# Graph-network kernel, attention pass: the next group's query-row matmuls go ahead of the second half's strip sums on TensorE

## What is computed

```python
Q, K, V = (h @ Wq), (h @ Wk), (h @ Wv)            # 8 heads of 32
score = einsum('ehd,ehd->eh', Q[dst], K[src]) / sqrt(32)
score = score + relu(efeat @ W1 + b1) @ W2 + b2
ex    = exp(score - segment_max(score, dst)[dst])
alpha = ex / segment_sum(ex, dst)[dst]
out   = segment_sum(alpha[:, :, None] * V[src], dst)
x     = layernorm(x + out @ Wo + bo)
```

## Times and profile before

| | us |
|---|---|
| median of 3 executions | 3339.93 |
| lowest and highest of them | 3326.34, 3346.44 |
| the profiled execution, its own time | 3330.41 |
| its span, first to last instruction | 3328.6 |
| part of the span in which groups of the attention pass run | about 130 to 843.5 |

### The profile page before, as it was taken

One profiled execution on the slowest core, in us unless ns is written; L12 is line 12 of the kernel. 1 busy time (PEld: TensorE's weight loads), 2 busy tenths in 40 slices (PEclk: granted clock), 3 DMA queues, 4 the chain that ended last, 5 costly groups with the idle time before them and its releaser, 6 DMA issues.

```text
span 3328.6 us, 64436 instructions
## 1 busy us (share of the span) xinstructions
PE 2517.7 (76%) x18326; PEld 1946.3 (58%) x18430; DVE 1968.7 (59%) x6179; ACT 685.5 (21%) x1593; POOL 1739.7 (52%) x1779
## 2 busy tenths in 40 slices
PE   7688888887556555567667675777777799999997
PEld 6344444444355555555555554666566488888875
DVE  3498988888655555466666666676777511111222
ACT  3244444444100000101111111111111311111110
POOL 0476555553377777677777775777777100000000
PEclk9899999999587878778888887898888799999998
DMA  5898777774133333333333332333333123322221
GB/s 188 247 267 243 218 211 213 216 214 133 53 108 110 110 109 110 99 106 114 117 118 106 116 117 79 121 117 117 121 114 120 65 99 104 103 98 91 92 91 62
DMA packets 185642, 435.94 MB, mean 131 GB/s; under 512 B 42868, under 2 KB 89322, under 8 KB 185578
## 3 DMA queue, kind: packets, MB, share of 16 engines
q0 software_dynamic: 93184, 272.74, 28.3%
q1 hardware_dynamic: 88794, 159.17, 14.8%
q10 hardware_dynamic: 3600, 3.28, 0.3%
HBM read 390.51 MB, written 44.51 MB: 131 GB/s over the span
## 4 chain that ended last, share of the span: by engine, by line
PE 32%; POOL 25%; issue 20%; DVE 12%; DMA 6%; DVEq 1%; ACT 1%; SPq 1%; POOLq 0%; ACTq 0%
POOL gath L769 25%; PE banks L1417 17%; PE banks L1260 4%; DMA gath<-h_table,idx_slot 3%; PE banks L1307 2%; PE banks L1243 2%; DVE prod L1758 2%; PE banks L1318 1%; PE banks L1083 1%; PE banks L1195 1%; DVE rh L1762 1%; PE banks L1319 1%; DVE rh L1786 1%; PE banks L1246 1%; DMA misc<-counts 1%
## 5 line engine op out<-in xcount | busy, mean ns | idle before, releaser
L769 POOL DMA_INDIRECT gath<-h_table,idx_slot x1248 | 1285.0, 1030 | 371.2 <-issue 342.3
L1260 PE MATMUL banks<-onehot,gath 128*128 128x128 f32 x4992 | 776.2, 322 | 458.1 <-DMA gath<-h_table,idx_slot 429.9
L1260 PEld LDWEIGHTS banks<-onehot,gath 128*128 128x128 f32 x4992 | 725.7, 231 | 515.9 <-DMA gath<-h_table,idx_slot 424.4
L1417 PE MATMUL banks<-gath,misc 128*128 128x256 bf16 x1875 | 515.6, 275 | 0.0
L1417 PE MATMUL banks<-acc,misc 128*128 128x256 bf16 x2500 | 419.7, 276 | 21.3 <-DMA misc<-counts 12.0
L1318 PE MATMUL banks<-gath 128*128 128x512 bf16 x624 | 251.5, 426 | 75.0 <-DVE gath L1964 74.8
L1417 PEld LDWEIGHTS banks<-acc,misc 128*128 128x128 bf16 x2500 | 242.5, 98 | 68.5 <-issue 16.1
L767 POOL DMA_INDIRECT rh<-kv_table,idx_slot x208 | 218.5, 1050 | 121.9 <-PE banks L1234 66.5
L767 POOL DMA_INDIRECT gath<-kv_table,idx_slot x208 | 211.0, 1014 | 124.0 <-PE banks L1234 68.5
L1964 DVE TENSOR_SCALAR gath<-w_qkv 128x800 bf16<-128x800 f16 x728 | 257.3, 422 | 0.0
L1844 DVE TENSOR_TENSOR acc<-acc,banks 128x256 f32 x156 | 65.0, 417 | 324.3 <-PE banks L1260 323.9
(11 more groups left out here) (218 smaller groups left out, 3421.6 us busy)
## 6 DMA issues: line engine op xcount, KB each, us to landing
misc<-counts SPq DMA_DIRECT2D x75, 800.0 KB, 4.3
counts<-misc SPq DMA_DIRECT2D x26, 800.0 KB
gath<-h_table,idx_slot POOLq DMA_INDIRECT x1248
rh<-in_dst_rows SPq DMA_DIRECT2D x106, 128.0 KB
w_qkv<-in_ef_t SPq DMA_DIRECT2D x106, 128.0 KB
q_win<-q_table SPq DMA_DIRECT2D x210, 64.0 KB
rh<-mask_dram SPq DMA_DIRECT2D x424, 8.0 KB
kv_table<-onehot SPq DMA_DIRECT2D x25, 256.0 KB, 2.0
```

Of the source, the lines that this page charges most:

```text
L769: pool.indirect_dma_start(row_slot[:, k, t, :], None, source, row_index).then_inc(gath_done[k][t // HALF], 16)
L1260: last = nc.tensor.matmul(banks[:, 3 * k + c, 0:P], row_slot[:, k, t, c * P:(c + 1) * P], onehot[:, k, t, :], start=(t == 0), stop=(t == T ...
L1417: last = nc.tensor.matmul(banks[:, slot, 0:D], c_slot[:, slot, c, :], parts[n % 2][j][:, c, :], start=(c == 0 and j == 0), stop=(c == NB - ...
```

## The change

On TensorE the first half's Q rows of group g + 1 are issued directly behind `turn_scores(g)`, ahead of the second half's strip sums of chunk g - 1, and no longer directly behind these. No instruction is added or removed, and the lists of all other engines stay as they were.

```diff
                     if not isinstance(g, int) or g < CHUNKS:
                         turn_scores(g, k, i)
+                    if full:
+                        q_rows(g + 1, 0)
                     if value:
                         tile_sums(g - 1, kc, 1)
                     if full:
-                        q_rows(g + 1, 0)
                         scores_back(g + 1, kn)
                     if not isinstance(g, int) or g < CHUNKS:
                         turn_weights(g)
```

## The result

| | before | after |
|---|---|---|
| median of 4 executions each | 3343.18 us | 3379.23 us |
| lowest to highest | 3326.34 to 3356.79 | 3369.42 to 3387.16 |
| ratio | | 1.0099, 95% interval 1.0072 to 1.0125 |
| attention pass in the trace, first L1208 to the end of the last window sums | 132.0 to 848.1, 716.1 us | 132.0 to 892.5, 760.4 us |
| span of the profiled execution | 3328.6 us | 3383.2 us |

By the ratio the change costs 1.0%, 33 us (the two medians lie 36 apart); the prediction had 28. A later comparison gave 1.0097 (1.0075 to 1.0119). Ratios leave out an execution that is over 1.5% above the fastest of its kernel; among all runs here that is one, in experiment 3. In the traces the attention pass is 44.3 us longer, in a second pair of traces (experiment 6) 25.4 us; what comes behind it took 2480 before and 2491 after in the first pair.

The account below looks back on a forecast made before the run. VectorE, 90% busy in the attention pass, was taken as nearly the bound. 16.3 us for full-clock and 11.6 for half-clock groups made +27.9, say 28, on the mean 3335.8: 3364 us, 8-in-10 range 3342 to 3390.

Parts of the forecast that it names:

- The chain: Full-clock group: Q rows end 1.75, strip sums 2.34, copy 3.10; exponent 3.12 instead of 2.63, `add_chunk` 5.59 instead of 5.10.
- The term of 16.3 us for 34 groups: Full-clock attention groups: exponent later by 0.49 in 21 groups and by 0.46 in 13 of kind k = 3.
- The k = 3 groups: Last group of a loop body: Q rows can't start before 1.14; exponent 3.68 instead of 3.22, +0.46, 13 groups.
- the term of 11.6 us: 17 attention groups with TensorE at 1.2 GHz: 12 lose 0.8 us each, 5 lose 0.4.
- my own signs of being wrong: L854 still at 2.63 in full-clock groups, granted clock leaving 0.94 by over 0.02, or VectorE waiting for gathers.
- The clock rival: Added idle drops 13 to 26 more groups to 1.2 GHz: 18 to 36 us extra, 3382 to 3400; chance 0.17.
- The groups between: Groups with 0.52 idle ahead of L1208, which might also fall to 1.2 GHz and lose 1.4 each.
- The other rivals: Attention pass: a gain of up to 19.8 us, 3316, chance 0.08; nothing moves, 3336 within 8, chance 0.11.
- The gain of up to 19.8: Attention pass: only VectorE's removed waits for Q rows stay, up to -19.8 us, 3316; chance 0.08.
- GpSimd's longer waits: Gathers waiting for second-half strip sums start 1.2 to 2 us later: no cost; +60 if their lead were gone.

Follow-up runs that it names:

- experiment 3: Changed order with the exponent ahead of the copy on ScalarE: ratio to the kernel before 1.0004; with five idle-time matmuls in even groups too, 0.9971.
- experiment 6: Change made in the hardware loop alone (groups 12 to 51): ratio to the kernel before 1.0092; changed kernel again 1.0097; kernel before traced again.
- experiments 1 and 2: Five idle-time matmuls behind the edge network's scores of each even group: in the old order ratio 0.9908, in the changed order 0.9977, both to the kernel before.
- the better order of the real ones: Old order with the edge network's score turn moved behind the window sums and the block's product: ratio to the kernel before 0.9945.

## Why the prediction was right, and where it was off

*The chain.* Each step is in the trace: Q rows behind L1208 at 0.61, at 1.14 in each fourth group, strip sums ending at 2.36 (2.34), L868 at 2.45 (2.42), an exponent with its input ready and no idle time ahead of it, L1215 bound by it in all groups, and a wait of L1821 for L1246 in 43 groups instead of 10. The forecast that a removed wait comes back at another place, larger, holds.

*Size at full clock: too large.* I had the exponent start 0.02 behind the copy's end, and so +0.49. It starts 0.11 ahead of that end (478.59 against 478.70), as L869 starts ahead of L868's end in the same rows. That makes +0.38, and the groups show +0.33 to +0.37. The term of 16.3 us for 34 groups was 11 to 12. The k = 3 groups came as the others did (+0.31), by the exponent, although TensorE idles 0.7 for the one-hot matrix there.

*Size at half clock: too small.* I took the stretch of half clock as given and put +0.8 or +0.4 on such a group. Measured is +1.3 to +1.65. The order's own 0.33 is 6 us of that in 17 groups. The rest is clock: the passes stand 22 and 28 above their order with the added matmuls before, 50 and 37 after, in the mean 18 more, and the timed medians give 13. So the term of 11.6 us was about 19 to 24. The two errors nearly cancel: with 11 to 12 for the full-clock groups this makes 30 to 36, for the 33 timed. That 28 came so close is in part luck.

*The signs.* One of my own signs of being wrong came true: the granted clock of the pass left 0.94 by 0.05 in the first trace, not by 0.02 at most; in the second it stood at 0.92. So of the two parts of the loss I had the chain of waits right and the clock wrong. I had also put the wait of L1215 for L854 at 50 us or more, and it came to 35.3: a full-clock group has 0.73 of it, a half-clock group 0.45. And VectorE was not "never late" before: it waited for the window sums in 10 groups.

*The clock rival.* It had the right resource and the wrong place. The groups between did not fall to 1.2 GHz. Nor did they get 0.5 of idle more: with the same work at the same clock, the added idle time is what the group grew by, 0.33 to 0.37. What grew is the length of the halved stretch, mostly 3.4 us before and mostly over 10 after, into the window sums. In the group shown the added wait of TensorE for the exponent, 0.45, lies within it. That this added idle time is what keeps the clock down is argued from the rows and from experiment 3, where an earlier L1215 went with half-clock groups of 14.2 in the one trace there is; it was not tested alone. That the idle time ahead of L1208 brings the halving is shown by experiments 1 and 2, where filling it removed all of them. So the section of the Trainium skill that I weighed, HAM oscillation in "TensorE: Matmul & The Clock Gate", names waits longer than what suffices here: the gap in the earlier trace rows is 1.69.

*The other rivals.* The gain of up to 19.8 was there on its own line (5.9 left) and was given back with more. GpSimd's longer waits cost nothing: no wait of L1759 for a gather over 0.9.

## What to carry to other kernels

Moving a step ahead in one engine's queue moves what it passes back by as much, so the question is who waits for that, and what stands behind it in the waiting engine's queue; here ScalarE had 0.76 us to spare and its input came 1.25 later. And where TensorE waits a lot but is on the path as soon as it works, look at its granted clock first: a few matmuls in the idle time gave 0.9%, and the better order of the real ones 0.55%, with intervals that overlap.

## What the runs showed of the hardware that I had not expected

Five 128x128 float32 matmuls in an idle time of 1.7 us took the half-clock groups of the attention pass from 17 to none in the traces of experiments 1 and 2. Of the four other traces with these matmuls, two have none in groups 8 to 50 and two have one each (group 15). Neighbouring ScalarE instructions overlap by 0.1 us in the records. And the executions of one kernel spread by over 1% in one comparison (3310.64 to 3351.67 for the kernel before, 27 executions).
